# Gate and up products of a routed FFN: native fp32 in place of three fp32r products of high and low parts

## The reference

```python
scores = sigmoid(xf @ gate_w.T)            # 64 experts
...                                        # top 4 of 8 groups, top 8 experts a token
cw = zeros((T, E)).at[rows, topk_idx].add(topk_w)
for Wg, Wu, Wd, w in experts:              # Wg, Wu: 176 x 256, Wd: 256 x 176
    g = xf @ Wg.T
    u = xf @ Wu.T
    y = y + (silu(g) * u) @ Wd.T * w[:, None]
return y + shared_out                      # a dense FFN of width 352 for all tokens
```

## Time and profile before

| | |
|---|---|
| median of 3 runs | 434.1 us (429.84, 434.1, 436.46) |
| span of the profiled execution | 431.7 us (2.4 us under the median) |
| granted PE clock, mean over the span | 0.911 of full speed |
| PE busy | 291.6 us (68%) |
| POOL busy | 279.0 us (65%) |
| DVE busy | 243.1 us (56%) |
| ACT busy | 211.8 us (49%) |
| expert loop, first gather in it to last scatter | 124.2 to 414.6 us |

### The profile page before, as it was taken

How to read it: one execution, slowest core, us unless ns; L and a number is a source line. 1 busy time by engine, 2 the same in 40 slices (tenths; PEclk the granted TensorE clock), 3 DMA queues, 4 the chain that set the end, 5 groups by cost and what they waited for, 6 DMA issues and landing times.

```text
span 431.7 us, 8449 instructions
## 1 busy us (share of the span) xinstructions
PE 291.6 (68%) x1483; PEld 229.6 (53%) x1484; DVE 243.1 (56%) x796; ACT 211.8 (49%) x505; POOL 279.0 (65%) x220
## 2 busy tenths in 40 slices
PE   0003597999999777777867667688777787877200
PEld 0001553555788656666756555667666566665200
DVE  3998798980467454556555545364554454555300
ACT  1433332381068564566556546475665465665300
POOL 6052203221558888888888888888888888888840
PEclk9999999895789898899899999898998899999855
DMA  7500020134256756677687788989657676654545
GB/s 237 203 0 1 1 99 0 24 100 150 66 138 128 144 91 132 132 166 137 113 197 168 165 197 190 218 184 210 132 88 169 155 166 149 133 91 84 84 63 86
DMA packets 35830, 53.86 MB, mean 125 GB/s; under 512 B 5452, under 2 KB 27628, under 8 KB 35820
## 3 DMA queue, kind: packets, MB, share of 16 engines
q0 software_dynamic: 17968, 28.65, 36.5%
q1 hardware_dynamic: 17852, 25.11, 18.9%
HBM read 38.90 MB, written 15.89 MB: 127 GB/s over the span
## 4 chain that ended last, share of the span: by engine, by line
PE 27%; issue 21%; DMA 17%; POOL 11%; DVE 5%; ACT 3%; POOLq 2%; ACTq 0%; DVEq 0%
DMA rows<-xfw,gidx 12%; PE bank L1050 7%; POOL rows L271 5%; PE bank L978 4%; PE bank L1087 4%; PE bank L1025 4%; PE bank L990 3%; POOL out L496 3%; POOL acc L496 3%; DMA out<-early_cq,sidx 3%; PE bank L1044 2%; DMA acc<-early_cq,sidx 2%; PE bank L1073 2%; PE bank L963 1%; ACT gu_hi L308 1%
## 5 line engine op out<-in xcount | busy, mean ns | idle before, releaser
L271 POOL DMA_INDIRECT rows<-xfw,gidx x90 | 106.0, 1178 | 43.2 <-issue 18.0
L312 DVE TENSOR_TENSOR gu_lo<-early_c,gu_hi 128x704 fp32r<-128x704 f32 x87 | 77.7, 893 | 37.1 <-ACT gu_hi L308 18.0
L1087 PE MATMUL bank<-d_ring,early_c 88*128 x336 | 93.5, 403 | 0.4 <-ACT early_c L595 0.4
L1044 PE MATMUL bank<-ident,rows 128*128 128x128 f32 x172 | 37.9, 305 | 65.5 <-DMA rows<-xfw,gidx 64.4
L496 POOL DMA_INDIRECT out<-early_cq,sidx x42 | 70.0, 1666 | 13.4 <-issue 12.7
L496 POOL DMA_INDIRECT acc<-early_cq,sidx x42 | 69.9, 1664 | 12.8 <-issue 11.6
L318 DVE TENSOR_TENSOR r_lo<-bank,r_hi 128x256 fp32r<-128x256 f32 x86 | 36.4, 424 | 68.8 <-ACT r_hi L292 51.5
L1044 PEld LDWEIGHTS bank<-ident,rows 128*128 128x128 f32 x172 | 21.2, 150 | 91.1 <-DMA rows<-xfw,gidx 85.7
L308 ACT ACTIVATE gu_hi<-early_c 128x704 fp32r x87 | 67.9, 782 | 0.0
L1087 PEld LDWEIGHTS bank<-d_ring,early_c 88*128 88x128 f32 x336 | 63.0, 204 | 8.2 <-issue 0.9
L1050 PE MATMUL bank<-gu_hi,r_hi 128*128 128x352 f32 x170 | 64.8, 381 | 0.9 <-DVE r_lo L318 0.9
(11 more groups left out here) (180 smaller groups left out, 340.0 us busy)
## 6 DMA issues: line engine op xcount, KB each, us to landing
early_c<-w_gu SPq DMA_DIRECT2D x37, 352.0 KB
d_ring<-w_down SPq DMA_DIRECT2D x36, 176.0 KB
rows<-xfw,gidx POOLq DMA_INDIRECT x90
xc<-x SPq DMA_DIRECT2D x2, 512.0 KB, 4.1
xc<-ctx_kn SPq DMA_DIRECT2D x1, 1024.0 KB, 8.4
acc<-zeros POOLq DMA_DIRECT2D x1, 1024.0 KB
xfw<-xf SPq DMA_DIRECT2D x1, 1024.0 KB, 4.4
out<-acc POOLq DMA_DIRECT2D x1, 1024.0 KB, 9.0
```

Of the source, the lines that this page charges most:

```text
L271: pool.indirect_dma_start(out=rows[:, r, :], out_offset=None, in_=xfw, in_offset=bass.IndirectOffsetOnAxis(ap=gidx[:, r:r + 1], axis=0), b ...
L312: v.tensor_tensor(gu_lo[:, b:b + 1, :], gu_ring[:, bass.ds(nth % R, 1), :], gu_hi[:, b:b + 1, :].bitcast(fp32), ALU.subtract).then_inc(glo ...
L1044: ins = pe.transpose(XT[b][:, k * P:(k + 1) * P], rows[:, r, k * P:(k + 1) * P], ident[:, :])
L1087: ins = pe.matmul(OB[b][:, 0:H], iT[:, b, s, :], d_ring[:, place, s, :], start=(s == 0), stop=(s == 1))
```

## The change

The high and low parts go. The rows of a slot are copied once, by DVE, from the PSUM bank to a tile `rT` (`keep_rows`), and `gate_up` multiplies them by the weights where they landed in `gu_ring`, two native fp32 products in place of six fp32r products. `gate_up` itself now waits for the announcement of the weights and for the row copy, and PE keeps register tables of its own for the place in the ring. SP refills a place of the ring upon `gu_ps` (the gate and up products are done) in place of `glo_ok` (the low part is made).

```diff
@@ -180,10 +180,7 @@
-        r_hi = sb("r_hi", [P, 2, KB, P], fp32r)
-        r_lo = sb("r_lo", [P, 2, KB, P], fp32r)
-        gu_hi = sb("gu_hi", [P, 2, KB * GU], fp32r)
-        gu_lo = sb("gu_lo", [P, 2, KB * GU], fp32r)
+        rT = sb("rT", [P, 2, KB, P])
...
@@ -287,9 +283,10 @@
-        def rows_high(act, b):
-            act.activation(r_hi[:, b, :, :], XT[b][:, 0:H].rearrange("p (k t) -> p k t", k=KB), ACT.Copy).then_inc(rhi_ok, 1)
+        def keep_rows(v, b, count):
+            v.wait_ge(rT_ps, count)
+            v.tensor_copy(rT[:, b, :, :], XT[b][:, 0:H].rearrange("p (k t) -> p k t", k=KB)).then_inc(rT_ok, 1)
...
@@ -298,25 +295,10 @@
-        def weights_high(act, nth, b):
-            act.activation(gu_hi[:, b:b + 1, :], gu_ring[:, bass.ds(nth % R, 1), :], ACT.Copy).then_inc(ghi_ok, 1)
-        def weights_low(v, nth, b, count):
-            v.wait_ge(ghi_ok, count)
-            v.tensor_tensor(gu_lo[:, b:b + 1, :], gu_ring[:, bass.ds(nth % R, 1), :], gu_hi[:, b:b + 1, :].bitcast(fp32),
-                            ALU.subtract).then_inc(glo_ok, 1)
-        def rows_low(v, b, count):
-            v.wait_ge(rhi_ok, count)
-            v.tensor_tensor(r_lo[:, b, :, :], XT[b][:, 0:H].rearrange("p (k t) -> p k t", k=KB), r_hi[:, b, :, :].bitcast(fp32),
-                            ALU.subtract).then_inc(rT_ok, 1)
...
@@ -390,7 +372,7 @@
-            sp.wait_ge(glo_ok, first)
+            sp.wait_ge(gu_ps, first)
...
@@ -399,7 +381,7 @@
-                        sp.wait_ge(glo_ok, first_next)
+                        sp.wait_ge(gu_ps, first_next)
...
@@ -574,35 +556,15 @@
             act.wait_ge(regs_ok, 1)
             quads = quads_of(act)
-            for f in range(2):
-                act.wait_ge(gu_there, (nth & (E - 1)) + 1)
-                weights_high(act, nth, f)
-            for f in range(2):
-                act.wait_ge(rT_ps, f + 1)
-                rows_high(act, f)
             act.wait_ge(gu_ps, 1)
             act.activation(silu[:, 0, :], GB[0][:, 0:I], ACT.Silu).then_inc(silu_ok, 1)
-            act.wait_ge(gu_there, (nth & (E - 1)) + 1)
-            weights_high(act, nth, 0)
             def quad(i):
                 for r in range(R):
                     act.wait_ge(iT_ps, i * R + (r + 1))
                     act.activation(iT[:, r % 2, :, :], IT[r % 2][0:I0, 0:2 * P].rearrange("p (s t) -> p s t", s=2),
                                    ACT.Copy).then_inc(iT_ok, 1)
-                    act.wait_ge(rT_ps, i * R + (r + 3))
-                    rows_high(act, r % 2)
-                    act.wait_ge(gu_there, (nth & (E - 1)) + 1)
                     act.wait_ge(gu_ps, i * R + (r + 2))
                     act.activation(silu[:, (r + 1) % 2, :], GB[(r + 1) % 2][:, 0:I], ACT.Silu).then_inc(silu_ok, 1)
-                    weights_high(act, nth, (r + 1) % 2)
                     act.wait_ge(acc_in[r % 2], i * (16 * R // 2) + 16 * (r // 2 + 1))
                     act.wait_ge(out_ps, i * R + (r + 1))
...
@@ -890,30 +850,23 @@
             for c in range(HC, C):
                 vector_out(v, c)
-                if c < HC + 2:
-                    weights_low(v, number(v, first_nths[c - HC]), c - HC, c - HC + 1)
             for f in range(2):
-                v.wait_ge(rT_ps, f + 1)
-                rows_low(v, f, f + 1)
+                keep_rows(v, f, f + 1)
                 copy_weight(v, number(v, first_experts[f]), f)
                 v.tensor_copy(gidx[:, f:f + 1], idx_tab[:, R + f:R + f + 1]).then_inc(gidx_ok, 1)
             combine(v, 0, 1)
-            weights_low(v, number(v, first_nths[2]), 0, 3)
             def quad(i):
                 for r in range(R):
                     g = (r + 2) % R
-                    v.wait_ge(rT_ps, i * R + (r + 3))
-                    rows_low(v, r % 2, i * R + (r + 3))
+                    keep_rows(v, r % 2, i * R + (r + 3))
                     copy_weight(v, number(v, experts[r]), g)
                     combine(v, (r + 1) % R, i * R + (r + 2))
                     v.tensor_copy(gidx[:, g:g + 1], idx_tab[:, bass.ds(i * R + (r + AHEAD), 1)]).then_inc(gidx_ok, 1)
                     v.wait_ge(acc_in[r % 2], i * (16 * R // 2) + 16 * (r // 2 + 1))
                     v.tensor_copy(sidx[:, r:r + 1], idx_tab[:, bass.ds(i * R + r, 1)]).then_inc(sidx_ok, 1)
-                    nth = number(v, nths[r])
-                    weights_low(v, nth, (r + 1) % 2, i * R + (r + 4))
             loop_over_quads(v, quads, quad)
...
@@ -1044,22 +997,24 @@
                     ins = pe.transpose(XT[b][:, k * P:(k + 1) * P], rows[:, r, k * P:(k + 1) * P], ident[:, :])
                 ins.then_inc(rT_ps, 1)
-            def gate_up(b):
-                parts = [(gu, r, k) for k in range(KB) for gu, r in ((gu_hi, r_hi), (gu_lo, r_hi), (gu_hi, r_lo))]
-                for s, (gu, r, k) in enumerate(parts):
-                    ins = pe.matmul(GB[b][:, 0:GU], r[:, b, k, :], gu[:, b, k * GU:(k + 1) * GU],
-                                    start=(s == 0), stop=(s == len(parts) - 1))
+            def gate_up(b, nth, count):
+                place = bass.ds(nth % R, 1)
+                pe.wait_ge(gu_there, (nth & (E - 1)) + 1)
+                pe.wait_ge(rT_ok, count)
+                for k in range(KB):
+                    ins = pe.matmul(GB[b][:, 0:GU], rT[:, b, k, :], gu_ring[:, place, k * GU:(k + 1) * GU],
+                                    start=(k == 0), stop=(k == KB - 1))
                 ins.then_inc(gu_ps, 1)
             pe.wait_ge(tabs_ok, 1)
             for f in range(2):
                 pe.wait_ge(row_in[f], 16)
                 turn_rows(f, f)
-            pe.wait_ge(glo_ok, 1)
-            pe.wait_ge(rT_ok, 1)
-            gate_up(0)
-            nths = four_registers(pe, "pe_nth")
-            pe.load(nths, nth_tab[0:1, 0:R])
+            downs, gus, first_nths = (four_registers(pe, n) for n in ("pe_down", "pe_gu", "pe_first_nth"))
+            pe.load(first_nths, nth_tab[0:1, 0:R])
+            pe.load(downs, nth_tab[0:1, 0:R])
+            pe.load(gus, nth_tab[0:1, 1:R + 1])
+            gate_up(0, number(pe, first_nths[0]), 1)
             quads = quads_of(pe)
             def quad(i):
                 for r in range(R):
...
@@ -1073,15 +1028,14 @@
                         ins = pe.transpose(IT[b][0:I0, s * P:(s + 1) * P], inter[:, b, s * I0:(s + 1) * I0], ident[:, :])
                     ins.then_inc(iT_ps, 1)
-                    pe.wait_ge(glo_ok, i * R + (r + 2))
-                    pe.wait_ge(rT_ok, i * R + (r + 2))
-                    gate_up((r + 1) % 2)
-                    nth = number(pe, nths[r])
+                    gate_up((r + 1) % 2, number(pe, gus[r]), i * R + (r + 2))
+                    nth = number(pe, downs[r])
                     place = bass.ds(nth % R, 1)
                     pe.wait_ge(down_there, (nth & (E - 1)) + 1)
                     if r == R - 1:
-                        pe.load(nths, nth_tab[0:1, bass.ds(i * R + R, R)])
+                        pe.load(downs, nth_tab[0:1, bass.ds(i * R + R, R)])
+                        pe.load(gus, nth_tab[0:1, bass.ds(i * R + (R + 1), R)])
                     pe.wait_ge(iT_ok, i * R + (r + 1))
                     for s in range(2):
                         ins = pe.matmul(OB[b][:, 0:H], iT[:, b, s, :], d_ring[:, place, s, :], start=(s == 0), stop=(s == 1))
```

More of the change, by code:

```diff
@@ L222, in xattn_moe_kernel @@
         gidx_ok, sidx_ok = sem("gidx_ok"), sem("sidx_ok")
-        rhi_ok, ghi_ok, glo_ok = sem("rhi_ok"), sem("ghi_ok"), sem("glo_ok")
         rT_ps, rT_ok, gu_ps, silu_ok, inter_ok, iT_ps, iT_ok, out_ps, y_ok = (
@@ L299, in four_registers, with load_quad @@
             return [eng.alloc_register(f"{name}{r}") for r in range(R)]
-        def load_quad(eng, registers, quad, numbers_only=False):
-            part = quad_tab[0:1, bass.ds(quad, 1), (1 if numbers_only else 0):2, :]
+        def load_quad(eng, registers, quad, which):
+            part = quad_tab[0:1, bass.ds(quad, 1), which:which + 1, :]
             eng.load(registers, part.rearrange("p q a r -> p (q a r)"))
-        def weights_high(act, nth, b):
-            act.activation(gu_hi[:, b:b + 1, :], gu_ring[:, bass.ds(nth % R, 1), :], ACT.Copy).then_inc(ghi_ok, 1)
-        def weights_low(v, nth, b, count):
-            v.wait_ge(ghi_ok, count)
-            v.tensor_tensor(gu_lo[:, b:b + 1, :], gu_ring[:, bass.ds(nth % R, 1), :], gu_hi[:, b:b + 1, :].bitcast(fp32),
-                            ALU.subtract).then_inc(glo_ok, 1)
-        def rows_low(v, b, count):
-            v.wait_ge(rhi_ok, count)
-            v.tensor_tensor(r_lo[:, b, :, :], XT[b][:, 0:H].rearrange("p (k t) -> p k t", k=KB), r_hi[:, b, :, :].bitcast(fp32),
-                            ALU.subtract).then_inc(rT_ok, 1)
         def copy_weight(v, e, r):
@@ L576, in _ @@
             quads = quads_of(act)
-            nths, first_nths = four_registers(act, "act_nth"), four_registers(act, "act_first_nth")
```

(29 more changed lines are left out.)

## The result

The changed kernel takes 420.94 us (median of 4 runs, 419.37 to 422.35) against 432.87 us before (median of 4, 429.84 to 436.46), a ratio of 0.9725 with a 95% interval of 0.9662 to 0.9787: faster. That is 11.9 us between the medians. On another chip it was 434.9 to 418.92 us, 0.9656 (0.9607 to 0.9705). The span of the profiled execution fell from 431.7 to 417.6 us, by 14.1.

The account below looks back on a forecast made before the run. POOL, running gathers and scatters back to back, was taken to bound the kernel. Terms of -15.5, 0, 0, 0, -0.3 and +0.8 gave -15.0 us: span 431.7 to 416.7, median 419.1 us, ratio 0.965, range 413 to 427.

Parts of the forecast that it names:

- What bounds the kernel: In the expert loop, POOL's gathers and scatters run back to back at 3.46 us a slot and never wait for PE.
- weights_low goes: Dropping DVE's line 312 subtraction in the loop removes all excess length of POOL's gathers and scatters: -15.5 us, at most.
- keep_rows comes: DVE's new row copy from PSUM in each slot costs POOL 0, at most 2.2 us.
- gate_up on PE: Two native products in each slot take 1.21 us against 1.04; 14 us over the loop, hidden under POOL's slot.
- Waits: PE's new waits for weights and row copy, and later ring refills, cost 0 in the loop, up to 3 us.
- The way in: At the entry to the loop, its first gather comes 0.3 us earlier, between -1.5 and +1.
- The faster scatters: With faster POOL, about a dozen scatters in the loop wait for the previous landing in their buffer: +0.8 us, 0 to +3.
- The sum: All terms together take 15.0 us off the program's span, from 431.7 to 416.7 us; median of runs 419.1 us.
- The rivals: Three other outcomes for the loop: scatter round trip 0.08, nothing freed (434 us) 0.06, PE bound 0.05.
- PE as the bound: Native products make PE's slot too long to cover half clock in the loop: over 437 us, 471 reckoned; chance 0.05.
- The round trip of the scatters: Scatters' landings in the loop take over as the limit, giving back 10 us: 429 us, range 424 to 431; chance 0.08.
- the list of signs: Expected loop profile: gathers 1.06 us, scatters 1.60, gaps 0.30, loop 275 us, PE's waits for landing rows smaller but still largest.

## Why the prediction was right, point by point

- *What bounds the kernel*: right. POOL ran back to back before and does so now but for five short waits, and its durations are what changed. (The prediction counts one pair of scatters with a longer gap in the kernel before; there are two, at 264.29 and 278.42.)
- *weights_low goes, -15.5 us*: measured -15.8 in POOL's busy time. Its cause is shown from both sides, by putting such an instruction into the changed kernel and by taking line 312 out of the kernel before.
- *keep_rows comes, 0 (up to 2.2)*: 0. The copy takes 425 ns, the 424 of line 318; 15 POOL instructions began under it and none is longer. That an input in PSUM makes a DVE instruction harmless is shown by the pair of added subtractions. For copies there is only the SBUF copy of 128x1024 beside this smaller one, so it is argued there.
- *gate_up on PE*: hidden, as forecast, but mis-sized. Timeline of PE in the changed kernel, the way in and one slot:

```profile
118.08 1.45 PE L1005 MATMUL bank<-early_c,rT 128*128 x4 [1.79 <-DVE rT L289]
...
120.97 1.45 PE L1005 MATMUL bank<-early_c,rT 128*128 x4
122.25 1.03 PE L1041 MATMUL bank<-d_ring,early_c 88*128 x4
123.11 0.38 PE L997 MATMUL bank<-ident,rows 128*128 128x128 f32 x2
123.34 0.38 PE L1028 MATMUL bank<-ident,early_t 128*88 128x128 f32 x2
123.71 1.45 PE L1005 MATMUL bank<-early_c,rT 128*128 x4
124.99 1.03 PE L1041 MATMUL bank<-d_ring,early_c 88*128 x4
125.85 0.38 PE L997 MATMUL bank<-ident,rows 128*128 128x128 f32 x2
```

```profile
125.95 0.38 PE L1073 MATMUL bank<-ident,early_t 128*88 128x128 f32 x2
```

(The second fence is the kernel before, in the slot of the earlier trace rows.) The products take 124.99 - 123.71 = 1.28 us from start to next start (forecast 1.21, bounds 1.04 to 1.42). But the slot is 125.85 - 123.11 = 2.74 us, not 2.44. The term left out two things: from the start of line 1028's transposes to the first product pass 123.71 - 123.34 = 0.37 us, where in the kernel before the same transposes (line 1073) and the first product start 0.13 us apart, and once a quad, in the slot with the two register tables, PE is idle for about 1 us. (That the tables cause it is argued from their place; no run takes them out of the loop. The kernel before loads one table there, and its six products take 1.05 us in the last slot, median, as in the other three.) With them PE has an estimated 0.24 us a slot in hand, by the run with three products, not the 0.83 (3.27 - 2.44) of the prediction. So PE's stretch was hidden with less room than forecast.
- *Waits*: 0 for the rings, as forecast; the trace names no wait of PE for weights.
- *The way in, -0.3 us*: measured -0.1. The three register loads do not stand beside the row copy as written; the first products began at 118.08, 0.63 later than before, and the run with early loads shows that the loads are the cause. What made up for it was luck: the prediction put the second products of the loop at half clock, 2.4 us, and they ran at full clock, 122.25 - 120.97 = 1.28 us (granted clock 1.00 there, 0.50 at the same place before). Counted from the program's first gather, the loop's first gather came 0.1 us later than before, not earlier.
- *The faster scatters, +0.8 us*: POOL's idle time in the loop without the wait for the first gather was 51.5 us and is 30.0 + 13.9 + 13.5 - 3.96 - 0.6 = 52.8, so +1.3, with five gaps over 0.4 us where there were two.
- *The sum*, -15.0 us: -14.1 in the span (416.7 forecast, 417.6 measured), and 419.1 us forecast against 420.94 measured. The profiled execution took 419.37 us, and the rest lies within the spread of the runs, 419.37 to 422.35. The medians fell by 11.9 us, less than the forecast's 15.0, and on the other chip by 16.0. (The range's upper end, 427, is a little low by its own terms: 419.1 and the four costs make 428.3.)
- *The rivals*: none came true. PE as the bound needed a third product. The round trip of the scatters shows in the five gaps, the longest 1.03 us. What the list of signs had wrong is that PE's largest wait would still be for landing rows: at 12.2 us it is below the 19.0 of its own register loads.

## What to carry to other kernels

Where an engine runs back to back with gaps that never change, compare its instructions' durations with their shortest: the spread is the gain, and what runs on the other engines at the start of the long ones names the cause. If GpSimd issues gathers and scatters and sets the pace, keep DVE instructions with two SBUF inputs and plain SBUF copies out of its way, or give one of their inputs in PSUM. One of 704 columns a slot added 13.6 us to POOL's durations and one of 352 columns 2.5, so splitting a long one should help; that estimate, two times 2.5 us against 13.6, was not run. And work that is taken off engines with time to spare gives nothing by itself: here six products became two, and ACT in the loop lost nearly half of its load (168.7 to 91.6 us), for no us.

## What the runs showed of the hardware

- A DVE subtraction with two SBUF inputs that is running when a GpSimd gather or scatter begins lengthens it by what is left of the subtraction less 0.13 us (in the run with two inputs put back 36 of 43 starts under it were longer, by 0.05 to 0.68 us, and each excess is this rule's to 0.04 us; in two of the other seven both began at the same instant, and in the kernel before one gather that began 0.04 us after the subtraction was not held up, while the subtraction took 0.97 us in place of 0.89). One of 0.89 us that begins while the gather or scatter runs lengthened none in 66 cases, and took 0.92 us at most.
- With one input in PSUM: nothing, in 41 starts under it.
- A copy of 128x1024 fp32 from SBUF to SBUF (0.70 us) does the same at the start, and if it still runs when the gather or scatter comes to its end, that waits too and ends 0.08 to 0.12 us after it.
- A scatter whose predecessor into the same accumulator landed late began 0.90 to 0.97 us after that landing (five in the changed kernel, nine without line 312); a gather that waited for its indices began 0.88 to 0.92 us after their copy had ended (73 of 84 with three products).
- Two native fp32 products of 352 columns took 1.28 us from start to next start at the full clock of 2.4 GHz, six fp32r products 1.04 us.
